# Two transformer layers: residual, normalisation and weight preparation in joined stages, absorbed weights kept in fp32

## The reference

```python
x = x + _layernorm(_L0_attn_ref(_layernorm(x), ...))     # 16 heads of 32, rotary, causal
x = x + _layernorm(_L0_ffn_ref(_layernorm(x), ...))      # silu(x Wg) * (x Wu), Wd; hidden 2048
x = x + _layernorm(_L1_attn_ref(_layernorm(x), ...))     # latent attention, below
x = x + _layernorm(_L1_ffn_ref(_layernorm(x), ...))      # ternary weights, rms norm of the hidden
# _L1_attn_ref, per head (16 heads, NOPE 128, ROPE 64, VD 128):
q = rmsnorm(h @ q_a_w.T, q_a_ln_w) @ q_b_w.T             # latent 384 -> 16 x (128 + 64)
ckv, k_pe_raw = split(h @ kv_a_w.T)                      # 128, 64
kv = rmsnorm(ckv, kv_a_ln_w) @ kv_b_w.T                  # 128 -> 16 x (128 + 128)
scores = (q_nope . k_nope + rope(q_pe) . rope(k_pe)) * SCALE
out = softmax(causal(scores)) @ v;  return out @ o_w.T
```

## Time and profile before

| | us |
|---|---|
| median of 3 runs (3184.61 to 3186.84) | 3185.22 |
| the profiled execution | 3187.83 |
| its span in the trace | 3186.0 |
| TensorE busy | 2862.2 (90%) |
| VectorE busy | 1879.3 (59%) |
| ScalarE busy | 1231.7 (39%) |
| GpSimd busy | 990.2 (31%) |

### The profile page before, as it was taken

One profiled execution on the slowest core, in us unless ns is written; L12 is line 12 of the kernel. 1 busy time (PEld: TensorE's weight loads), 2 busy tenths in 40 slices (PEclk: granted clock), 3 DMA queues, 4 the chain that ended last, 5 costly groups with the idle time before them and its releaser, 6 DMA issues. The chain is left out here.

```text
span 3186.0 us, 42804 instructions
## 1 busy us (share of the span) xinstructions
PE 2862.2 (90%) x14636; PEld 2289.0 (72%) x14636; DVE 1879.3 (59%) x3604; ACT 1231.7 (39%) x2366; POOL 990.2 (31%) x780
## 2 busy tenths in 40 slices
PE   7969999789999999458999999857999999499998
PEld 5846666568787878347788888656888888378886
DVE  5647787574453545445566666655666666644446
...
GB/s 165 239 212 142 121 129 125 56 142 83 42 64 41 64 24 34 212 291 74 18 23 35 23 23 35 29 140 28 24 23 35 23 23 30 126 21 20 10 37 80
DMA packets 138035, 244.06 MB, mean 77 GB/s; under 512 B 14417, under 2 KB 78929, under 8 KB 137393
## 3 DMA queue, kind: packets, MB, share of 16 engines
...
## 5 line engine op out<-in xcount | busy, mean ns | idle before, releaser
L1094 POOL TENSOR_TENSOR l0a_probs_hl<-l0a_probs,l0a_probs_hl 128x896 fp32r<-128x896 f32 (+1 forms) x128 | 285.0, 2244 | 108.1 <-ACT l0a_probs L1022 108.1
L1352 ACT ACTIVATE l1a_probs<-l1a_scores,l1a_row 128x128 f32<-128x128 f32 (+7 forms) x256 | 189.6, 742 | 317.9 <-DVE l1a_row L1389 317.8
L1326 PE MATMUL l1a_obank<-l1a_pT_hl,l1k_v_hl 128*128 128x512 f32 (+3 forms) x1152 | 300.4, 370 | 7.2 <-DVE l1a_pT_hl L1399 7.1
L1442 POOL TENSOR_TENSOR l1a_q_stage<-l1k_qpe,l1a_ones 128x512 fp32r<-128x512 f32 x32 | 33.3, 1041 | 875.3 <-PE l1a_work L1334 818.4
L1399 DVE TENSOR_TENSOR l1a_pT_hl<-l1a_work,l1a_pT_hl 128x512 fp32r<-128x512 f32 (+3 forms) x384 | 213.2, 555 | 154.6 <-ACT l1a_pT_hl L1359 154.4
L1306 PE MATMUL l1a_scores<-l1k_kT_hl,l1a_qa_hl 128*128 128x512 f32 (+3 forms) x1152 | 291.6, 361 | 1.5 <-ACT l1a_probs L1352 1.5
L1359 ACT CAST l1a_pT_hl<-l1a_work 128x512 fp32r<-128x512 f32 (+3 forms) x384 | 183.7, 478 | 106.3 <-PE l1a_work L1317 105.2
L1334 PE MATMUL l1a_work<-l1a_wov,l1a_oT_hl 128*128 128x512 f32 x768 | 214.3, 401 | 5.0 <-DVE l1a_oT_hl L1418 3.0
L1389 DVE TENSOR_REDUCE l1a_row<-l1a_scores 128x1 f32<-128x128 f32 (+7 forms) x256 | 190.0, 751 | 44.5 <-PE l1a_scores L1309 44.4
L1413 DVE SCALAR_TENSOR_TENSOR l_acc<-l1a_work,l1a_row,l_acc 128x512 f32<-128x512 f32 x256 | 189.4, 750 | 34.4 <-PE l1a_work L1334 24.5
L1713 PE MATMUL f0f_ybank<-f0f_wT,f0f_h_hl 128*128 128x512 f32 x768 | 196.7, 406 | 12.7 <-POOL f0f_h_hl L1879 12.6
...
## 6 DMA issues: line engine op xcount, KB each, us to landing
...
qk_dram<-l0f_stage SPq DMA_DIRECT2D x128, 128.0 KB, 2.5
l1a_wov<-wov_dram SPq DMA_DIRECT2D x32, 512.0 KB, 3.4
l0a_v_stage<-v_dram SPq DMA_DIRECT2D x32, 384.0 KB, 4.3
l1a_wabs<-wabs_dram SPq DMA_DIRECT2D x32, 384.0 KB, 3.8
l0a_q_stack<-qk_dram SPq DMA_DIRECT2D x32, 256.0 KB, 3.6
l0a_k_stack<-qk_dram SPq DMA_DIRECT2D x32, 256.0 KB, 3.8
f0f_chunk<-in_L_ffn_w_gate_up SPq DMA_DIRECT2D x32, 256.0 KB, 2.7
```

The source lines that it names most:

```text
L1094: nc.gpsimd.tensor_tensor(probs_hl[:, r, 1, 0:wide], probs[:, r, 0:wide], f32(probs_hl[:, r, 0, 0:wide]), ALU.subtract).then_inc(low_done, 1)
L1326: last = pe.matmul(obank[:, c:SPAN], src["v_hl"][:, a, n, :], pT_hl[:, ring(n, s), b, c:SPAN], start=(n == 0 and i == 0), stop=(n == QT * ...
L1352: nc.scalar.activation(probs[s][:, first:first + wide, :].rearrange("p k c -> p (k c)"), scores[:, n % S_AHEAD, 0:wide * P], ACT.Exp, bias ...
```

## The change

1. `residual_and_weights` becomes `residual_norm_and_weights`: the sum goes back into `acc`, no ring z; x is loaded in pairs of tiles; the 8 tiles of batch row 0 are also normalised, transposed and split into xT (`xT1`), beside the jobs. Rotary tables and norm weights are loaded here. wabs and wov leave as one fp32 array each. The stage `l1n` of row 0 is gone.
2. The attentions load these arrays and split them: event U (wabs) and V (wov), a copy on ScalarE and a subtraction on GpSimd.
3. `l1r` of row 0 is gone; the latent stage of row 1 does this residual (`rows`), one tile a step. `l_acc` lives through both rows.
4. `l1r` of row 1 and `f1n` become one stage, `residual_norm_transposed`: A tiles are rows of batch row 0 (loaded from x3), B tiles those just added.
5. `f1f` scales and adds in `acc` in place of a tile z.

```diff
+def join_order():
+    order = [("A", k) for k in range(QT)]
+    for k in range(TB - QT):
+        order += [("A", QT + k), ("B", k)]
+    return order + [("B", k) for k in range(TB - QT, TB)]
...
+def residual_norm_transposed(nc, m, ident, done_rows, acc, src, dst, xT_hl, loads):
...
+            for tile, rows, loaded in ((x0, done_rows, x0_loaded), (x1, src, x1_loaded)):
+                for g in range(2):
+                    sp.dma_start(tile[:, g * QT:(g + 1) * QT, :],
+                                 rows[g * SPAN:(g + 1) * SPAN, :].rearrange("(t p) d -> p t d", p=P)).then_inc(loaded[g], 16)
+            for tile, extra in loads:
+                sp.dma_start(tile, extra).then_inc(next_loaded, 16)
+            for k in range(TB):
+                sp.wait_ge(sum_done, k + 1)
+                sp.dma_start(dst[k * P:(k + 1) * P, :], acc[:, k, :]).then_inc(stored, 16)
...
+            for i in range(N + LATER + 4):
+                j = i - LATER
+                if i < TB:
+                    statistics(0, i, acc[:, i, :])
+                if 0 <= j < N:
+                    kind, k = order[j]
+                    if kind == "A":
+                        dve.wait_ge(x0_loaded[k // QT], 16)
+                    else:
+                        dve.wait_ge(sum_done, k + 1)
+                    statistics(1, j, source(j))
+                if 0 <= i - 1 < TB:
+                    inverse(0, i - 1)
+                if 0 <= j - 1 < N:
+                    inverse(1, j - 1)
+                if i < TB:
+                    aggregate(0, i)
+                if 0 <= j < N:
+                    aggregate(1, j)
+                if 0 <= j - 4 < N:
+                    j = j - 4
+                    dve.wait_ge(high_done, j + 1)
+                    nc.vector.tensor_tensor(xT_hl[:, 1, :, tokens(j)],
+                                            bank[:, j % RING, :].rearrange("p (k t) -> p k t", k=KT),
+                                            f32(xT_hl[:, 0, :, tokens(j)]), ALU.subtract).then_inc(low_done, 1)
...
+            for i in range(N + LATER + 4):
+                if 0 <= i - 1 < TB:
+                    root(0, i - 1)
+                if 0 <= i - LATER - 1 < N:
+                    root(1, i - LATER - 1)
+                if 0 <= i - 2 < TB:
+                    k = i - 2
+                    scaled(0, k, acc[:, k, :], acc[:, k, :]).then_inc(z_done, 1)
+                if 0 <= i - LATER - 2 < N:
+                    j = i - LATER - 2
+                    wait(act, turned, j - 1)
+                    scaled(1, j, xn[:, j % 2, :], source(j)).then_inc(normed, 1)
+                if 0 <= i - LATER - 4 < N:
+                    j = i - LATER - 4
+                    act.wait_ge(turned, j + 1)
+                    nc.scalar.copy(xT_hl[:, 0, :, tokens(j)], bank[:, j % RING, :].rearrange("p (k t) -> p k t", k=KT)
...
+        ev.append(("U", h + 2, 0, 0))
+    if s == 1 and more(h + 1):
+        ev.append(("V", h + 1, 0, 0))
...
+    ev += [("U", 0, 0, 0), ("U", 1, 0, 0), ("V", 0, 0, 0)]
...
-                sp.wait_ge(x_high, 2 * (h - 1))
-            sp.dma_start(f32(wabs[:, par]), src["wabs_dram"][bass.ds(h, 1)].rearrange("o p a k c -> p (o a) k c")
+                sp.wait_ge(wabs_low, h - 1)
...
-                sp.wait_ge(o_high, 2 * h - 1)
-            sp.dma_start(f32(wov[:, par]), src["wov_dram"][bass.ds(h, 1)].rearrange("o p a c -> p (o a) c")
+                sp.wait_ge(wov_low, h - 1)
+            sp.dma_start(wov_raw[:, par], src["wov_dram"][bass.ds(h, 1)].rearrange("o p c -> p (o c)")
...
-                            pe.wait_ge(wabs_loaded[hp], 16 * (it * (HB // 2) + h // 2 + 1))
+                            pe.wait_ge(wabs_low, head_of(it, h) + 1)
...
-                        pe.wait_ge(wov_loaded[hp], 16 * (it * (HB // 2) + h // 2 + 1))
+                        pe.wait_ge(wov_low, head_of(it, h) + 1)
...
+                elif kind == "U":
+                    act.wait_ge(wabs_loaded[hp], 16 * (it * (HB // 2) + h // 2 + 1))
+                    nc.scalar.copy(wabs[:, hp, 0], wabs_raw[:, hp]).then_inc(wabs_high, 1)
+                elif kind == "V":
+                    act.wait_ge(wov_loaded[hp], 16 * (it * (HB // 2) + h // 2 + 1))
+                    for i in range(WORK):
+                        wait(act, work_full[i], seen[i])
+                    nc.scalar.copy(wov[:, hp, 0], wov_raw[:, hp]).then_inc(wov_high, 1)
...
+                elif kind == "U":
+                    hp = h % 2
+                    pool_wait(wabs_high, head_of(it, h) + 1)
+                    nc.gpsimd.tensor_tensor(wabs[:, hp, 1], wabs_raw[:, hp], f32(wabs[:, hp, 0]), ALU.subtract
...
-                        sp.dma_start(dst[n * P:(n + 1) * P, :], z[:, t, :]).then_inc(row_stored[t], 16)
+                        sp.dma_start(dst[n * P:(n + 1) * P, :], acc[:, n, :]).then_inc(row_stored, 16)
...
+                    nc.scalar.activation(acc[:, half * QT + b, :], acc[:, half * QT + b, :], ACT.Identity,
...
+def joined_steps(jobs):
+    for i in range(NT + 4):
+        yield i, (i - 5 if 0 <= i - 5 < jobs else None)
...
+def residual_norm_and_weights(nc, m, ident, src, dst, acc, w, waT, wpT, xT_hl, loads, wabs_dram, wov_dram):
...
+                rows = src[g * PAIR * P:(g + 1) * PAIR * P, :].rearrange("(t p) d -> p t d", p=P)
+                sp.dma_start(x[:, g % 2], rows).then_inc(x_loaded[g % 2], 16)
...
+                if g + 2 < NT // PAIR:
+                    load_rows(g + 2)
...
+            load_rows(0)
...
+            load_rows(1)
             for e in range(2):
                 sp.dma_start(qp[e * ROPE:(e + 1) * ROPE], w["qp"][e]).then_inc(pe_loaded, 16)
-            load_rows(1)
+            store_rows(0)
             load_q(0)
-            load_ow(0)
-            store_rows(0)
-            load_rows(2)
+            store_rows(1)
             sp.dma_start(k_b[:, :, :], w["k_b"]).then_inc(kb_loaded, 16)
-            store_rows(1)
-            load_rows(3)
-            sp.dma_start(v_b[:, :, :], w["v_b"]).then_inc(vb_loaded, 16)
-            load_q(1)
-            load_ow(1)
             store_rows(2)
             store_rows(3)
+            sp.dma_start(v_b[:, :, :], w["v_b"]).then_inc(vb_loaded, 16)
+            store_rows(4)
+            load_q(1)
+            store_rows(5)
+            load_ow(0)
+            store_rows(6)
+            load_ow(1)
+            store_rows(7)
             load_q(2)
+            for tile, extra in loads:
+                sp.dma_start(tile, extra).then_inc(next_loaded, 16)
...
+            for i, j in joined_steps(J):
+                if 0 <= i - 1 < NT:
+                    root(0, i - 1)
+                if 0 <= i - 5 < TB:
+                    root(1, i - 5)
+                if 0 <= i - 2 < NT:
+                    scaled(0, i - 2, acc[:, i - 2, :]).then_inc(z_done, 1)
+                if j is not None:
+                    blocks, view, hi, lo = jobs[j]
+                    act.wait_ge(job_turned, j + 1)
+                    nc.scalar.copy(hi, view(bank[:, slot_of["J", j]])).then_inc(job_high, 1)
+                if 0 <= i - 6 < TB:
+                    t = i - 6
+                    wait(act, x_turned, t - 1)
+                    scaled(1, t, xn[:, t % 2, :]).then_inc(normed, 1)
...
+                nc.scalar.activation(wabs[:, h % 2], abank[:, h % 2, 0:3 * P].rearrange("p (j c) -> p j c", j=3),
+                                     ACT.Copy, scale=SCALE1).then_inc(a_read, 1)
...
+            for i, j in joined_steps(J):
+                if i < NT:
+                    statistics(0, i)
+                if 0 <= i - 4 < TB:
+                    dve.wait_ge(sum_done, i - 3)
+                    statistics(1, i - 4)
+                if 0 <= i - 1 < NT:
+                    inverse(0, i - 1)
+                if 0 <= i - 5 < TB:
+                    inverse(1, i - 5)
+                if i < NT:
+                    aggregate(0, i)
+                if 0 <= i - 4 < TB:
+                    aggregate(1, i - 4)
+                if j is not None:
+                    blocks, view, hi, lo = jobs[j]
+                    dve.wait_ge(job_high, j + 1)
+                    nc.vector.tensor_tensor(lo, view(bank[:, slot_of["J", j]]), f32(hi), ALU.subtract).then_inc(job_low, 1)
...
+                nc.vector.tensor_copy(wov[:, h % 2], vbank[:, h % 2, :]).then_inc(v_read, 1)
...
+def latent_operands(nc, m, ident, xT_hl, waT, wpT, norm_w, rope, out, stores=(), rows=None):
...
+                for t in range(TB):
+                    sp.wait_ge(r_sum_done, t + 1)
+                    sp.dma_start(row_dst[t * P:(t + 1) * P, :], acc[:, t, :]).then_inc(r_stored, 16)
+                    if t + 2 < TB:
+                        load_row(t + 2)
...
+                if rows is not None and 1 <= i <= TB:
+                    t = i - 1
+                    act.wait_ge(r_mv_done, t + 1)
+                    nc.scalar.activation(r_std[:, t % 2:t % 2 + 1], r_mv[:, t % 3, 1:2], ACT.Sqrt, bias=eps_ln[:, 0:1]
```

(36 more changed lines are left out.)

389 lines of the change are left out of this document (250 added, 139 removed).

## The result

| | before | changed |
|---|---|---|
| median, us | 3186.03 (4 runs, 3184.61 to 3194.3) | 3137.01 (4 runs, 3133.01 to 3140.14) |
| the profiled execution, us | 3187.83 | 3139.53 |
| its span, us | 3186.0 | 3137.8 |

The ratio is 0.9842, 95% interval 0.9823 to 0.9862: 49 us less, where 3135 was forecast and 3112 to 3160 was the range. The changed kernel is faster by more than 0.2%.

What follows compares the result with a forecast made beforehand. Limits taken by stage: attention by TensorE, weight stage by transfers, residual and normalisation stages by VectorE chains. Terms -41 + 6.4 - 19.4 + 16 - 13 = -51 from 3187.8, less 2.6, gave 3134; predicted 3135 us, range 3112 to 3160.

Steps and rivals of the forecast that it cites:

- Weight stage: Weight stage plus row 0's normalisation: 98 us in place of 139.0, so -41 us, bounds -50 to -27.
- The order: Weight stage timed step by step: rows end at 50 us, heads about 2.2 us each from 63, last store at 97.
- the byte rule: Weight stage time from bytes moved: 29.0 MB at 305 GB/s gives 95 us.
- rival A: Weight stage's row part is late, five pairs by 3 us each: 14 us longer, 3149 us; chance 0.14.
- Rival D: Weight stage heads wait for stores in turn, 6.8 us each: +62 us, 3197 us, kernel slower; chance 0.02.
- Attentions: Both layer-1 attentions: 0.9 us at the start and 2.3 in the loop each, +6.4 us, bounds +1.8 to +28.
- The term for the copies: Attention loop: 0.9 us of ScalarE copies less 0.74 slack costs 0.16 us a head, 2.3 us an attention.
- Rival B: Attentions do not absorb the splits: TensorE loses 0.9 us in 29 heads, 26 us, 3156 us; chance 0.10.
- Moved residual: Row 0's residual inside row 1's latent stage: +12 us in steps, +3.9 at the end, +16; bounds +8 to +20.
- The ring: Row 1's latent stage: VectorE shift, aggregate, ScalarE root, scaling, down copy and products close a loop; 10.3 us against 7.93 a tile.
- Rival C: Latent stage of row 1: the loop does not close because the shift gets through, 8 us less, 3127; chance 0.08.
- Joined stage: Last residual and layer 1's feed-forward normalisation as 22 steps: 43 us in place of 55.9, -13 us, bounds -17 and -7.

Runs made afterwards that it cites:

- e4: Changed kernel with wabs and wov stored and loaded as high and low parts again; ratio to the kernel before 0.9870, weight stage 108.8 us against 96.0.
- e8: Changed kernel with three buffers in place of two for the pairs of x rows; ratio to the kernel before 0.9843, weight stage 94.8 us against 96.0.
- e7: Changed kernel with four slots in place of two for absorbed weights on their way to DRAM; ratio to the kernel before 0.9845, weight stage 93.1 us.
- e3: Changed kernel with the raw wabs and wov copies moved behind T's third and fifth copy; ratio to the kernel before 0.9840, each attention 558.2 us.
- e10: Changed kernel with one more 128x512 copy ahead of wov's in every second attention unit; ratio to the kernel before 0.9891, attentions 569.8 and 568.3 us.
- e1: Changed kernel with reciprocal and shift moved ahead of the direct and crossed products; ratio to the kernel before 0.9830, down copies 8.35 us apart.
- e2: Changed kernel with all row work in row 1's latent stage moved off the ring; ratio to the kernel before 0.9817, down copies 7.95 us apart.
- e6: Kernel before with only the last residual and layer 1's feed-forward normalisation joined into one stage; ratio to the kernel before 0.9962.

## Why the prediction was right

The time came out 2 us from the forecast. Each step's mechanism was found as described; the sizes were off by 0 to 4 us, with errors that partly cancel.

**Weight stage, -41 forecast, -43.0.** The bytes were right (29.0 MB forecast; 303 GB/s x 96.0 us = 29.1), the end of the rows too (50 forecast, 48.6). The order came out too: the third head's store was issued at 62.7 us (63 forecast), and from there a head took 2.2 us (2.2 forecast). That the byte rule gave the same number was chance: the share of 0.63 behind 1360 shows that bytes do not bind to the end. Of the 43 us, e4 puts about 13 to the storage; the other 30 go to the rest of the new stage (the normalisation within the rows' part, no ring z, x in pairs), which no run takes apart. VectorE waited 5.6 us there for the sum, not 15: rival A did not occur, and e8 shows that earlier loads give nothing. Rival D, the heads at 6.1 us, did not occur either: they took 47.4 / 16 = 3.0 us, with the wait for W_o counted. Its mechanism, heads that wait for earlier stores, was there; e7 puts 3 us to it.

**Attentions, +6.4 forecast, +10.1.** The term for the copies, 0.9 - 0.74 = 0.16 us a head, measured 0.20, and e3 and e10 show the threshold on both sides. Rival B (all of 0.9) fell. The start was 4.21 us in place of 3.04, +1.2 where +0.9 was forecast. What is left over in row 0, some 3 us, is the clock: a first interval of 22.5 us in a window at 0.87 (21.1 before, 19.9 in e1) and an end of 4.6 us in place of 3.0. In row 1 the same first interval went the other way, from 21.3 us before to 19.9, and the way to it took 2.1 us more in place of 1.1; so +3.4, close to the 3.2 forecast, is partly luck.

**Moved residual, +16 forecast, +17.0.** The ring was named with its members and closed. A step took 9.95 where 10.3 was added up: from the end of crossed to the copy of down 3.5 us in place of 3.85. The first two intervals grew by 1.4 and 1.5 us, which had not been counted. The end grew by 4.2 (3.9 forecast), of which 3.3 lie behind the last qpe addition; the rest comes with a group of 18 matmuls at 5.93 us in place of 4.36. The upper bound, +20 for all eight steps, had left this end out; with it the sum gives +23, and nothing came near it. Rival C fell with the shift at 1.79 us. e1 takes the shift's wait out of the ring, 1.6 us of the step; what e2 moved beyond that (statistics, aggregate, root, scaling, the order on GpSimd) is the other 0.4, not taken apart.

**Joined stage, -13 forecast, -11.2.** 44.7 us with the clearing, 43 forecast, and e6 shows it alone.

**Not forecast:** +1.3 us in the latent stage of row 0, where one group of 18 matmuls took 5.98 us in place of 4.45 by the clock, and -3.0 before the weight stage. Luck has a part in the net: the terms sum to -45.2, 6 us short of the -51 forecast, and the 3.0 us of scatter ahead of the stage make up half of that.
